# The order of SP's transfers during attention: each batch's maxima issued ahead of one expert's weights, in place of four experts first

## What is computed

```python
x = x + attention(layernorm(x), ctx, ctx, lens)     # softmax(s * q^T k) v for each head
y = layernorm(x)
probs = softmax(y @ Wg); e = argmax(probs)          # one expert of 8 for each token, 128 rows each at most
out = (silu(rows_e @ W1[e]) * (rows_e @ W3[e])) @ W2[e]
shared = (silu(y @ sw1) * (y @ sw3)) @ sw2
x = x + gate * out + shared
```

## Time and profile before

| | |
|---|---|
| median of 3 runs | 194.24 us (193.72 to 194.97) |
| the profiled execution | 194.63 us, span of its instructions 192.7 us |
| mean granted TensorE clock | 0.886 of full speed |
| busy, share of the span | PE 83%, DVE 54%, ACT 44%, POOL 33% |
| queue q1 (SP's transfers) | 14.98 MB, 25.1% of 16 engines' span |

### The profile page before, as it was taken

How to read it: one execution, slowest core, us unless ns; L and a number is a source line. 1 busy time by engine, 2 the same in 40 slices (tenths; PEclk the granted TensorE clock), 3 DMA queues, 4 the chain that set the end, 5 groups by cost and what they waited for, 6 DMA issues and landing times.

```text
span 192.7 us, 3827 instructions
## 1 busy us (share of the span) xinstructions
PE 159.4 (83%) x1448; PEld 112.5 (58%) x1448; DVE 104.7 (54%) x241; ACT 84.6 (44%) x189; POOL 62.7 (33%) x85
## 2 busy tenths in 40 slices
PE   7679505999998999999999687299893999979960
PEld 7445103555545455555455387298792889779840
DVE  1497202525795978777341433423868238598530
ACT  2632000544747585665757363514751155465000
POOL 5158000092027081432202000044085058535241
PEclk9975555557999999999999999969999799999996
DMA  4999990000000000000070000002025845983001
GB/s 131 343 342 329 322 333 24 0 5 2 2 5 2 3 2 3 2 3 2 0 228 1 2 0 0 3 31 82 0 82 153 292 123 154 306 269 140 29 22 54
DMA packets 15697, 18.44 MB, mean 96 GB/s; under 512 B 1852, under 2 KB 14949, under 8 KB 15680
## 3 DMA queue, kind: packets, MB, share of 16 engines
q1 hardware_dynamic: 14240, 14.98, 25.1%
q0 software_dynamic: 1152, 2.97, 4.6%
q10 hardware_dynamic: 288, 0.26, 0.4%
HBM read 14.12 MB, written 4.21 MB: 95 GB/s over the span
## 4 chain that ended last, share of the span: by engine, by line
PE 62%; SPq 11%; DVE 10%; issue 4%; DMA 4%; POOL 3%; ACT 2%; another core or an unknown queue 2%; DVEq 0%; POOLq 0%; ACTq 0%
PE bank L919 12%; PE bank L940 9%; PE bank L956 8%; PE bank L1003 5%; PE bank L1005 4%; PE bank L1150 4%; DMA qz<-mrow 4%; PE bank L1080 3%; PE bank L1124 3%; PE bank L1125 3%; SPq L278 3%; PE bank L968 2%; SPq L305 2%; DVE xlo L639 2%
## 5 line engine op out<-in xcount | busy, mean ns | idle before, releaser
L500 DVE TENSOR_REDUCE nm<-bank 128x2 f32<-128x512 f32 x64 | 41.1, 685 | 27.4 <-PE bank L919 27.3
L940 PE MATMUL bank<-qz,kz 32*128 32x256 f32 x256 | 46.5, 443 | 9.2 <-DMA qz<-mrow 9.2
L919 PE MATMUL bank<-kz,qz 32*128 32x256 f32 x256 | 43.9, 472 | 2.1 <-POOL qz L358 1.5
L746 ACT ACTIVATE pt<-bank 128x512 f32<-128x512 f32 x64 | 34.6, 589 | 18.0 <-PE bank L940 17.9
L940 PEld LDWEIGHTS bank<-qz,kz 32*128 32x128 f32 x256 | 27.9, 204 | 15.7 <-issue 11.2
L919 PEld LDWEIGHTS bank<-kz,qz 32*128 32x128 f32 x256 | 25.8, 217 | 15.8 <-DVE nm L500 7.4
L956 PE MATMUL bank<-pt,vext 128*32 128x256 f32 x256 | 21.1, 406 | 0.0
L358 POOL TENSOR_SCALAR qz<-xs,rs,mrs 128x256 f32<-128x256 f32 x14 | 7.7, 565 | 39.4 <-DVE mrs L468 39.4
L420 POOL DMA_INDIRECT expert_rows<-rk,idx_s x8 | 8.1, 1012 | 32.6 <-DVE rk L586 30.8
L1150 PE MATMUL bank<-wraw,kz 128*128 128x256 f32 (+1 forms) x48 | 11.8, 386 | 1.8 <-DVE hTlo L646 1.4
L725 ACT COPY vext<-bank 128x256 f32<-128x256 f32 x8 | 3.0, 370 | 23.2 <-PE bank L896 23.2
(11 more groups left out here) (140 smaller groups left out, 316.7 us busy)
## 6 DMA issues: line engine op xcount, KB each, us to landing
wraw<-in_w SPq DMA_DIRECT2D x16, 352.0 KB, 7.5
wraw<-in_w SPq DMA_DIRECT2D x8, 256.0 KB, 7.5
expert_rows<-zero SPq DMA_DIRECT2D x1, 1032.0 KB, 10.3
out<-xs SPq DMA_DIRECT2D x8, 128.0 KB, 3.5
xs<-in_x SPq DMA_DIRECT2D x3, 256.0 KB, 6.1
cs<-in_ctx SPq DMA_DIRECT2D x3, 256.0 KB, 6.3
wraw<-in_w SPq DMA_DIRECT2D x8, 96.0 KB, 8.1
wraw<-in_sw SPq DMA_DIRECT2D x2, 352.0 KB, 4.5
```

The lines of the kernel that those rows point to most:

```text
L500: nc.vector.tensor_reduce(nm[:, b % 2, :, place], scores_bank[:].rearrange("p (u c) -> p u c", u=2), AX_X, ALU.max, negate=True).then_inc( ...
L746: nc.scalar.activation(pt[:, g % NPT, n % 4, :], sc_bank[n % NS][:], ACT.Exp).then_inc(exped, 1)
L919: mm = nc.tensor.matmul(scores_bank[:, u * D:(u + 1) * D], qz[rows, b, half, u * P:(u + 1) * P], kz[rows, b, half, :], start=True, stop=True)
L940: mm = nc.tensor.matmul(sc_bank[n % NS][:, c * D:(c + 1) * D], kz[rows, b, half, c * P:(c + 1) * P], qz[rows, b, half, :], start=True, sto ...
```

## The change

SP's list is written in another order. The maxima of batch b come first and the weights of expert b + 1 behind them, for b = 0 to 3; the fill of the expert rows comes behind the maxima of batch 4. `load_maxima(b)` waits for `nm_row` of its batch, so each expert is now issued after that wait. What is transferred, and into which slot, is the same, and nothing changes on the other engines.

```diff
-            for e in range(1, NW):
-                load_expert(e)
-            sp.wait_ge(empty_set, 2)
-            sp.dma_start(xd_dram.rearrange("(n p) d -> p n d", p=P),
-                         zero[:].unsqueeze(1).broadcast_to([P, E, DW])).then_inc(xd_zeroed, 16)
             for b in range(B):
                 load_maxima(b)
+                if b + 1 < NW:
+                    load_expert(b + 1)
+                if b + 1 == NW:
+                    sp.wait_ge(empty_set, 2)
+                    sp.dma_start(xd_dram.rearrange("(n p) d -> p n d", p=P),
+                                 zero[:].unsqueeze(1).broadcast_to([P, E, DW])).then_inc(xd_zeroed, 16)
             load_expert(0)
```

## The result

| | before | after |
|---|---|---|
| median | 193.98 us (4 runs, 192.56 to 194.97) | 180.34 us (4 runs: 176.32, 177.47, 183.22, 184.29) |
| ratio after / before | | 0.9124, 95% interval 0.9012 to 0.9236 |
| profiled execution | 194.63 us, span 192.7 | 177.47 us, span 174.6 |
| mean granted clock in it | 0.886 | 0.954 |

The account below looks back on a forecast made before the run. Bound: PE waits 9.25 us for the first maxima, queued behind weights and zeros. Removing that, other terms 0, takes 194.63 to 185.4, or 185.0 against the median of 194.24; range 182.5 to 187.3 us.

Parts of the forecast that it names:

- The pause: PE's wait for batch 0's maxima, held up by SP's queue: the whole stall goes, -9.25 us.
- The landing: Batch 0's maxima land at 19.6 us, before PE needs them at 21.79: no stall, bound 0.9 us.
- Term 2: SP's new waits for rows of maxima: no later maxima or loads come late, 0 us.
- Term 3: Expert weights and zeros loaded beside attention: no instruction gets longer, 0 us, bounds 0 to +0.6.
- term 4: PE's clock: its rise moves along with the work from 46.1 to 36.9 us; no term, +-0.8 in the range.
- Rival (a): Without the pause PE's clock rises early: gain up to 3.9 us, taken as 2.6, giving 182.4; chance 0.08.
- Nothing was hidden in it: In the stall before the first L940 all four compute engines were idle, so its removal gives the whole 9.25 us.
- A gain beyond the stall is excluded here: PE's work before it needs the maxima at 21.79 us does not depend on them, so at most 9.25 us.

Follow-up runs that it names:

- a_again: The changed kernel once more with no edit; six executions took 176.66 to 184.93 us, the traced one 183.41 us.
- b_fill74: Kernel before the change with 74 x 4 small filler matmuls at the start in place of 50 x 4; median 192.84 us, ratio 0.998.
- b_mid: Kernel before the change with 48 full-array filler matmuls in PE's turns 2, 3 and 5 to 8; median 188.84 us, ratio 0.975.
- f74_m0: Changed kernel with 74 x 4 fillers at the start and only batch 0's maxima ahead of all four experts and the zeros; median 187.71 us.
- a_mid: Changed kernel with 48 full-array filler matmuls in PE's turns 2, 3 and 5 to 8; median 175.95 us, ratio 0.908 to the kernel before.
- a_fill20_2: Changed kernel with 20 x 4 filler matmuls at the start in place of 50 x 4, run again for a trace; 182.36 us.

## Why the prediction was right and wrong

**Right: what bounds, and what is removed.** The pause ended by the queue, and it went: 9.25 us became 0.15 to 0.21. The landing was taken as in time with a bound of 0.9; it took 2.5 us from row to use. *Term 2* held: no later wait of PE for maxima is in the trace, and the loads ended in time. *Term 3*, 0 with a bound of 0.6, measured 0.0 between the marks (61.54 against 61.56 us) and 0.3, within the spread, in the medians.

**Right only for some executions: term 4.** The rise of the clock was let to move along with the work, to 36.9 us. In the traced execution of `a_again` the last rise came at 35.5, and that kind, seven of ten, has a median of 183.4, inside the range. That is luck in part: as told above, its clock took another course on the way. In the traced one of the other three the clock was up from 11.7 us on. Rival (a) named this with a chance of 0.08. The step that failed is the reading of one trace's clock as a property of the order of work: "that order of work is unchanged, so I let the rise move along". The same list of instructions gave both. Nor does the rise need the weighing of values, as the prediction read it: at 11.7 us there was none. The Trainium skill ("TensorE: Matmul & The Clock Gate", "What's actually happening") says that the point of the transition depends on where in a free-running window the first matmul lands, and varies by 500 ns either way for it. That the point varies, these executions bear out; its size they do not: the first rise came at 11.7 us in one and at 18.5 in the other, which fell again. The kernel before could not show this, since its pause set the time of what followed, and in the traces of it and of `b_fill74` and `b_mid` the turns behind the pause began at 0.50.

**Wrong: the sizes.** Two terms were too small where the clock is up; even rival (a) at its full 3.9 would have given 185.0 - 3.9 = 181.1, not 177.
- "Nothing was hidden in it": the pause hid how long the early scores take. At full clock PE needs the maxima at 18.93, not 21.79, so 2.9 us more than the pause come back; `b_fill74`, where PE was ready at 18.86 and the pause grew to 12.35, shows the same from the other side. "A gain beyond the stall is excluded here" was false for that reason.
- Rival (a) priced four turns behind the pause at up to 3.9, by the pace of late turns, 2.21 us each. Late turns each weigh values, and hold the transposes of outputs and tokens (L969, L977 and L984 in the trace after). Of the four turns behind the pause only the last weighs values (L957 starts at 25.54 and 27.19), and they took 19.15 to 27.19, 8.04 us in place of 8.84: a gain of 4.7. And (a) stopped counting at 43.79, where the clock before was still at 0.50, until 46.2; up to the third row that gives 0.9 more, so 5.6.

For the profiled execution the sum would have been 194.63 - 9.25 - 2.9 + 0.2 - 5.6 = 177.1, measured 177.47. The span gained another 0.5 us behind the eighth row, which was not traced to a cause, and the time around the span is 2.9 us in place of 1.9; the two make the rest. For the other kind, 194.63 - 9.4 = 185.2, and 183.41 was measured: 0.7 more was gained up to the eighth row (94.77 to 84.66) and 1.3 after it.

**The range** took the clock as +-0.8 for one turn. It should have reached down to the whole of (a) with both sizes put right, near 177, since nothing in the trace spoke on how often the clock would rise. What stays open is why the clock falls or stays in one execution and not in another, near 8 and near 20 us; filler shows that PE's own work has a say in it, not why the rest differs.

## What to carry to other kernels
- A small transfer on which an engine waits belongs ahead of bulk loads on its queue, and the later small ones must not stand behind the bulk either: one batch ahead alone (`f74_m0`) only moved the pause. Spacing the bulk between them or putting it behind them all came to the same here (176.7 and 176.4 us).
- A pause whose end is set elsewhere hides how fast the work before it is, and here left PE at half clock behind it. Before costing its removal, cost both stretches at either clock, and forecast two values when one trace can't say which will hold.
- When a kernel's times spread after a change, look at the clock of each execution: a few tens of cheap matmuls in PE's sparse turns (`a_mid`) bought 6 us of median (on different chips), while the same in a kernel with the pause bought 5.

## What the runs showed of the hardware
- With one and the same kernel the clock fell between 8.2 and 8.4 us in two traces, in which PE had been idle from 5.8 us on, until 8.0 and until 8.5, and was back at 11.7 us in one and at 18.5 in the other. There it fell again at 21.9, after PE had been busy for 3.29 of 3.70 us, and stayed low for 13.6 us though PE was busy in all of them. Between the medians of the long and the short executions lie 6.7 us of 177.
- The recorded clock can be wrong for 10 us and more: 1.00 from 8 to 18 us in `a_fill20_2`, where pairs of transposes took 0.69 us and not 0.44. The Trainium skill warns in "TensorE: Matmul & The Clock Gate" ("Seeing it yourself") that such records have been seen to be unreliable; this trace agrees.
- Four experts' weights and the zero fill, 5.4 MB, loaded beside attention cost nothing that the traces show: 61.54 us with them and 61.56 without, from the first to the eighth row of maxima at a clock of 1.00.
